# The residual of a two-layer block: identity products against a copy through memory

## The reference

```
def reference(x, seq2, lengths, expert, ...):
    y = x + attention(x, seq2, lengths) @ Wo + bo            # layer 1
    h = gelu(y @ W1 + b1)                                    # exact Gelu, 2048 wide
    shared = h @ W2 + b2                                     # 384 columns
    own    = h @ We[expert] + be[expert]                     # 128 columns, by batch
    return y + concat([shared, own], axis=-1)                # layer 2
```

## Time and profile before

| | |
|---|---|
| Median of 3 runs | 1981.19 us (1977.24 to 1981.42) |
| The profiled execution | 1981.18 us |
| Its span, first to last instruction | 1979.3 us |
| Granted clock of TensorE, mean | 0.984 of full speed |
| PE busy | 1909.4 us (96%), 8032 products |
| DVE busy | 976.5 us (49%), 1437 instructions |
| ACT busy | 825.8 us (42%), 1418 instructions |
| DMA | 122.15 MB moved |

### The profile page before, as it was taken

The page is one execution under the profiler, slowest core; times in us unless marked ns, Lnnn a source line. Parts: engine busy times, 40 slices in busy tenths (PEclk is TensorE's granted clock), DMA queues, the critical chain, the costliest instruction groups (busy, mean ns, idle before and its releaser), DMA issues.

```text
span 1979.3 us, 25912 instructions
## 1 busy us (share of the span) xinstructions
PE 1909.4 (96%) x8032; PEld 1329.4 (67%) x8032; DVE 976.5 (49%) x1437; ACT 825.8 (42%) x1418; POOL 178.6 (9%) x140
## 2 busy tenths in 40 slices
PE   6999999999999999999999799999999999999997
PEld 5655655656556556556565368888888888888886
DVE  4576585675775775866756663323232323232311
ACT  3354455454454544554544544232323232323222
POOL 3021030030120210300200100000000000000000
PEclk8999999999999999999999879999999999999999
DMA  6151243332331512432321432221212121212111
GB/s 139 33 113 43 68 84 77 60 80 53 76 79 38 117 38 65 90 76 59 75 59 43 142 100 80 35 52 31 54 29 56 27 58 25 60 23 62 21 27 22
DMA packets 337243, 122.15 MB, mean 62 GB/s; under 512 B 285642, under 2 KB 304074, under 8 KB 337170
## 3 DMA queue, kind: packets, MB, share of 16 engines
q1 hardware_dynamic: 336658, 120.83, 28.4%
q10 hardware_dynamic: 512, 0.53, 0.2%
HBM read 53.63 MB, written 16.79 MB: 36 GB/s over the span
## 4 chain that ended last, share of the span: by engine, by line
PE 88%; DVE 5%; issue 3%; SPq 2%; ACT 1%; DMA 1%; POOL 0%; DVEq 0%; ACTq 0%
PE ps_proj L1109 17%; PE ps_av L1185 11%; PE ps_max L1139 6%; PE ps_av L1061 6%; PE ps_av L1063 6%; PE ps_av L1062 6%; PE ps_score L1173 6%; PE ps_proj L1061 3%; PE ps_max L1063 3%; PE ps_score L1063 3%; PE ps_max L1062 3%; PE ps_score L1062 3%; PE ps_score L1061 3%; PE ps_max L1061 3%; PE ps_proj L1062 3%; PE ps_proj L1063 3%
## 5 line engine op out<-in xcount | busy, mean ns | idle before, releaser
L618 ACT ACTIVATE p_f<-ps_score 128x512 f32<-128x512 f32 x512 | 305.2, 598 | 457.4 <-PE ps_score L1173 439.5
L838 DVE TENSOR_REDUCE m_col<-ps_max 128x1 f32<-128x512 f32 x512 | 332.3, 685 | 258.3 <-PE ps_max L1139 257.0
L994 DVE TENSOR_TENSOR h_lo<-h_f,h_hi 128x512 fp32r<-128x512 f32 x128 | 88.3, 690 | 481.2 <-ACT h_hi L729 481.1
L1185 PE MATMUL ps_av<-p_f,v_st 128*64 128x512 f32 x1024 | 255.5, 620 | 0.0
L1173 PE MATMUL ps_score<-stacks 99*128 99x512 f32 x512 | 216.6, 425 | 10.2 <-ACT p_f L618 10.2
L1109 PE MATMUL ps_proj<-in_hi,w_hi 128*128 128x512 f32 x512 | 208.4, 407 | 10.7 <-POOL in_lo L510 7.4
L1139 PE MATMUL ps_max<-stacks 97*128 97x512 f32 x512 | 185.9, 421 | 26.5 <-DVE m_col L838 19.2
L1109 PE MATMUL ps_proj<-in_lo,w_hi 128*128 128x512 f32 x512 | 207.6, 406 | 0.0
L1109 PE MATMUL ps_proj<-in_hi,w_lo 128*128 128x512 f32 x512 | 207.2, 405 | 0.0
L1061 PE MATMUL ps_av<-y_hi,w_hi 128*128 128x512 f32 x512 | 199.4, 390 | 1.5 <-DVE y_lo L990 1.5
L1063 PE MATMUL ps_av<-y_hi,w_lo 128*128 128x512 f32 x512 | 199.2, 389 | 0.0
(11 more groups left out here) (126 smaller groups left out, 2803.0 us busy)
## 6 DMA issues: line engine op xcount, KB each, us to landing
stacks<-parts SPq DMA_DIRECT2D x384, 128.0 KB
raw<-in_x_dram SPq DMA_DIRECT2D x128, 64.0 KB, 2.2
raw<-in_fside_BxSxS_dram SPq DMA_DIRECT2D x128, 64.0 KB, 2.2
attn_scratch<-num SPq DMA_DIRECT2D x32, 256.0 KB, 2.4
x_raw<-in_x_dram SPq DMA_DIRECT2D x128, 64.0 KB, 2.1
a_raw<-attn_scratch SPq DMA_DIRECT2D x32, 256.0 KB, 3.4
we_raw<-in_L_cond_We_dram SPq DMA_DIRECT2D x32, 256.0 KB, 2.8
out_dram<-z_t SPq DMA_DIRECT2D x128, 64.0 KB, 1.9
```

Of the source, the lines that this page charges most:

```text
L618: act.activation(p_f[:, i % FLIGHT], ps_score[i % 2][:, :], ACT.Exp, scale=SCALE).then_inc(p_made, 1)
L838: dve.tensor_reduce(m_col[:, n % C, n // C:n // C + 1], ps_max[n % 2][:, :], AX.X, ALU.max).then_inc(max_made, 1)
L994: dve.tensor_tensor(h_lo[:, m % 2], h_f[:, :], f(h_hi[:, m % 2]), ALU.subtract).then_inc(h_lo_made, 1)
L1185: pe.matmul(ps_av[j // 2][at:at + 2 * DH, :], v_st[:, t, HG * g + j, :], p_f[:, i % FLIGHT], start=(t == 0), stop=(t == C - 1)).then_inc(a ...
```

## The change

The identity products go. What they added comes in another way:

- SP stores each `y_f` in memory (`keep_residual`, into a new tensor `resid_scratch`, 256 KB a tile).
- SP fetches it into `z_f`, the buffer of the result (`fetch_residual`). The tiles 0 and 1 of a batch are fetched ahead; the tiles 2 and 3 when `z_f` is free, which is when the turn two tiles earlier has been done.
- DVE evicts the output bank with bias and residual in one operation, in place in `z_f` (`result` moves from ACT to DVE).
- The output banks are started by the first output product (`m` = 0), which now waits for `z_made`.
- `x_t` goes; x is turned into `y_f`, which has two buffers now. A turn of x waits for the store of the `y` two tiles earlier.

```
+            def keep_residual(b, c):
+                sp.wait_ge(y_f_made, C * b + c + 1)
+                sp.dma_start(resid_dram[bass.ds(b, 1), c].rearrange("o p s -> (o p) s"), y_f[:, c % 2]).then_inc(y_stored[c % 2], DMA)
+            def fetch_residual(b, c):
+                wait(sp, z_t_made, C * b + c - 1)
+                sp.wait_ge(y_stored[c % 2], DMA * (2 * b + c // 2 + 1))
+                sp.dma_start(z_f[:, c % 2], resid_dram[bass.ds(b, 1), c].rearrange("o p s -> (o p) s")).then_inc(y_back[c % 2], DMA)
...
+                if first:
+                    sp.wait_ge(w2_lo_made, W2S)
+                fetch_residual(b, 0)
+                fetch_residual(b, 1)
+                if not last:
                     residual(b + 1, 0)
                     expert_weights(b + 1, 1)
                     expert_weights(b + 1, 2)
                     for c in range(1, C):
                         residual(b + 1, c)
+                        keep_residual(b + 1, c - 1)
+                    keep_residual(b + 1, C - 1)
                 for c in range(C):
+                    if c + 2 < C:
+                        fetch_residual(b, c + 2)
                     result(b, c)
...
             def turn_x(b, c):
                 n = C * b + c
                 dve.wait_ge(x_landed, (P // QUAD) * DMA * (n + 1))
-                wait(dve, y_f_made, n)
-                dve.transpose(x_t[:, :], x_raw[:, :]).then_inc(x_made, 1)
+                wait(dve, y_lo_made, n - 1)
+                wait(dve, y_stored[c % 2], DMA * (2 * b + c // 2))
+                dve.transpose(y_f[:, c % 2], x_raw[:, :]).then_inc(x_made, 1)
...
+            def result(b, c):
+                dve.wait_ge(out_mm, KH * (b + 1))
+                if c == CS:
+                    dve.wait_ge(be_landed, DMA * (b + 1))
+                dve.wait_ge(y_back[c % 2], DMA * (2 * b + c // 2 + 1))
+                dve.scalar_tensor_tensor(out=z_f[:, c % 2], in0=ps_out[c][:, :], scalar=bias_2[:, c:c + 1],
+                                         in1=z_f[:, c % 2], op0=ALU.add, op1=ALU.add).then_inc(z_made, 1)
...
                 for c in range(C):
+                    result(b, c)
                     turn_result(b, c)
...
-                    pe.matmul(ps_out[c][:, :], ident[:, :], y_hi[:, c], start=True, stop=False)
-                    pe.matmul(ps_out[c][:, :], ident[:, :], y_lo[:, c], start=False, stop=False)
...
+                    if m == 0:
+                        wait(pe, z_made, C * (b - 1) + c + 1)
+                    mm = three(ps_out[c][:, :], left, (h_hi[:, m % 2], h_lo[:, m % 2]), m == 0, m == KH - 1)
```

More of the change, by code:

```diff
@@ L42, in cond_resid_program @@
     attn_dram = nc.dram_tensor("attn_scratch", (B, C, P, S), F32, kind="Internal").ap()
+    resid_dram = nc.dram_tensor("resid_scratch", (B, C, P, S), F32, kind="Internal").ap()
     mask_dram = nc.dram_tensor("mask_scratch", (B, S), F32, kind="Internal").ap()
@@ L139, in cond_resid_program @@
         x_raw = sb2("x_raw", [P, S])
-        x_t = sb2("x_t", [P, S])
+        y_f = sb2("y_f", [P, 2, S])
         a_hi = sb2("a_hi", [P, C, S], F32R)
@@ L144, in cond_resid_program @@
         y_lo = sb2("y_lo", [P, C, S], F32R)
-        y_f = sb2("y_f", [P, S])
         h_f = sb2("h_f", [P, S])
@@ L217, in cond_resid_program @@
         y_f_made, y_hi_made, y_lo_made = sem("y_f_made"), sem("y_hi_made"), sem("y_lo_made")
+        y_stored = [sem(f"y_stored{r}") for r in range(2)]
+        y_back = [sem(f"y_back{r}") for r in range(2)]
         h_mm = sem("h_mm")
@@ L441, in _ @@
             residual(0, 2)
+            keep_residual(0, 0)
             residual(0, 3)
+            keep_residual(0, 1)
             w2_piece(2)
@@ L445, in _ @@
             w2_piece(3)
+            keep_residual(0, 2)
             expert_weights(0, 2)
+            keep_residual(0, 3)
             for n in range(4, W2S):
@@ L720, in y_high @@
                 wait(act, h_mm, KH * b)
-                act.copy(y_hi[:, c], y_f[:, :]).then_inc(y_hi_made, 1)
+                act.copy(y_hi[:, c], y_f[:, c % 2]).then_inc(y_hi_made, 1)
             def hidden(b, m):
@@ L729, in hidden @@
                 act.activation(h_hi[:, m % 2], ps_av[m % 2][:, :], ACT.Gelu, bias=bias_1[:, m:m + 1]).then_inc(h_hi_made, 1)
[L731 to L738, removed]
             act.wait_ge(small_landed, 4 * DMA)
@@ L769, in rows @@
                         y_high(b + 1, c)
-                for c in range(C):
-                    result(b, c)
             batches(act, rows)
@@ L983, in y_out @@
                 dve.wait_ge(x_made, n + 1)
-                wait(dve, y_lo_made, n)
-                dve.scalar_tensor_tensor(out=y_f[:, :], in0=ps_proj[c % 2][:, :], scalar=bias_o[:, c:c + 1],
-                                         in1=x_t[:, :], op0=ALU.add, op1=ALU.add).then_inc(y_f_made, 1)
+                dve.scalar_tensor_tensor(out=y_f[:, c % 2], in0=ps_proj[c % 2][:, :], scalar=bias_o[:, c:c + 1],
+                                         in1=y_f[:, c % 2], op0=ALU.add, op1=ALU.add).then_inc(y_f_made, 1)
             def y_low(b, c):
                 dve.wait_ge(y_hi_made, C * b + c + 1)
-                dve.tensor_tensor(y_lo[:, c], y_f[:, :], f(y_hi[:, c]), ALU.subtract).then_inc(y_lo_made, 1)
+                dve.tensor_tensor(y_lo[:, c], y_f[:, c % 2], f(y_hi[:, c]), ALU.subtract).then_inc(y_lo_made, 1)
             def hidden_low(b, m):
@@ L1272, in hidden @@
                     mm.then_inc(h_mm, 1)
-            def residuals(b):
-                for c in range(C):
-                    wait(pe, z_made, C * (b - 1) + c + 1)
-                    pe.matmul(ps_out[c][:, :], ident[:, :], y_hi[:, c], start=True, stop=False)
-                    pe.matmul(ps_out[c][:, :], ident[:, :], y_lo[:, c], start=False, stop=False)
             def outputs(b, m, first):
@@ L1289, in outputs @@
                         pe.wait_ge(we_lo_made, 4 * b + m // 4 + 1)
-                    mm = three(ps_out[c][:, :], left, (h_hi[:, m % 2], h_lo[:, m % 2]), False, m == KH - 1)
+                    if m == 0:
+                        wait(pe, z_made, C * (b - 1) + c + 1)
+                    mm = three(ps_out[c][:, :], left, (h_hi[:, m % 2], h_lo[:, m % 2]), m == 0, m == KH - 1)
                 mm.then_inc(out_mm, 1)
@@ L1304, in rows @@
                     hidden(b, m, range(C - 1, C))
-                residuals(b)
                 for m in range(KH):
```

## The result

| | before | after |
|---|---|---|
| median of 6 runs each, us | 1979.55 (1977.24 to 1981.42) | 1998.38 (1997.42 to 2000.78) |
| ratio after / before, 95% | | 1.0101 (1.0090 to 1.0111) |
| profiled execution, us | 1981.18 | 2000.78 |
| its span, us | 1979.3 | 1999.0 |

The direction was forecast, the size was not: 1986.0 with a range up to 1994.0. The profiled execution after is the slowest of its six, by 2.4 us over the median.

The account below looks back on a forecast made before the run. TensorE, busy for 100.00 of 100 us in the second half, was taken to bound the kernel. First batch +0.4, seven changes of batch +3.5 and tail +0.9 gave +4.8 us on 1981.18: 1986.0, range 1978.5 to 1994.

Parts of the forecast that it names:

- What goes: TensorE loses eight residual products in each of eight batches, 1.86 us a batch: 14.9 us if nothing else were late.
- what is late next: At a change of batch hidden tile 2 waits for ACT's second Gelu of tile 0, about 0.83 us.
- The chain over DVE and SP: At seven changes of batch, results, SP's issues and the fourth turn delay the low half: +0.5 us each, +3.5 us.
- the transfers: Two 256 KB fetches among a batch's outputs push the eighth output by 0.2 us, between 0 and 0.83.
- P - R: From the start of a batch's first result (R) to the next batch's first output product (P): forecast 10.15 us.
- the last step: From the fourth turn to the start of the next batch's first output product: forecast 1.33 us.
- rival D: TensorE's waits drop its clock to the 1.2 GHz level at seven changes of batch: +24 us, 2005; chance 0.05.
- The first batch: Turns of x 2 and x 3 wait for the stores of y, so hidden tile 2 starts later: +0.4 us.
- The tail: Behind the last product, SP starts 0.13 later, the fourth output 0.55 later, plus 0.2 for the transfer: +0.9 us.
- A: DMAs cheap, only the two issues cost, and the first batch's stores land early: +2.7 us, 1984; chance 0.27.
- B: SP's issue and the fetches hide fully because the waits for z_t and y overlap: -6.7 us, 1974.5; chance 0.10.
- C: Fourth y's fetch lands late behind outputs; fourth turn 1.0 us later in seven places and tail: +12.8, 1994; chance 0.16.

Follow-up runs that it names:

- v2: v1 with hidden tile 0 done whole before tile 1 on TensorE, and the next batch's first low half made before the last two turns on DVE: 1965.97 us.
- x6b: The changed kernel with the two late fetches of a batch cut to 64 of 512 columns, issues still on SP: 1985.09 us, ratio 1.0033 to before.
- x5b: The changed kernel with the two late fetches of a batch issued by ACT instead of SP, bytes as they are: 1983.73 us, ratio 1.0027 to before.
- v1: The changed kernel with the third and fourth y fetched early, mid-batch, into a_raw, none between the outputs: 1973.32 us, ratio 0.9975 to before.

## Why the prediction was wrong, step by step

**What goes, and what is late next.** Right. The eight products were put at 1.86 us, and v2, which doesn't wait in a change of batch, is 1.87 faster a batch. The wait of hidden tile 2 for the Gelu was forecast at 0.83 and is 0.83 (1386.14 to 1387.20, less a pace).

**The chain over DVE and SP.** This is the step that failed, by the size of one term, the transfers. The mechanism is the forecast one: the two fetches push the eighth output, the fourth turn waits for it, the low half stands behind the turn, TensorE behind that. P - R was to be 10.15 us and is 10.91. The terms: issue 6.84 for 6.69, the transfer 2.65 for 2.13, the last step 1.42 for 1.33. So the term "I take 0.2" for the transfers, between 0 and 0.83, measured 0.69, near the upper end. Its reason, that work and issue time are almost equal, used the mean share of the engines over the stretch; but a fetch that is issued in the midst of outputs makes those behind it land late, also when the mean leaves room. x6b confirms it: with seven eighths of the bytes gone and the issues left, the chain is 10.15. With the landing later, a change of batch became +1.45 instead of +0.5. Of the 0.95 between them 0.76 are the chain's; most of the rest is one place, the first change: there the first result starts 1.3 us after the last output product instead of 0.4, since it stands on DVE behind the low half of the fourth y, and ACT, which made it before, had no such queue. The prediction had put the start of the result at no change.

```profile
1278.26 0.69 DVE L1005 TENSOR_TENSOR y_lo<-y_f,y_hi 128x512 fp32r<-128x512 f32 x1 [0.69 <-ACT y_hi L747]
1278.87 0.74 DVE L1017 SCALAR_TENSOR_TENSOR z_f<-ps_score,bias,z_f 128x512 f32<-128x512 f32 x1
```

Seven times 0.95 is +6.6 us over the forecast, 1992.6 by this alone, and with the clock's 9.6 us 2002.2; the profiled execution took 2000.78, with a first half that was 1.3 us shorter.

**The clock, rival D.** It was given 0.05 and came true in six of seven places, though at half its price: 1.6 us a place, 9.6 us for the 19 that the rival had, which took twelve slow products at each of seven places where there were 7 or 8 at six. The reason against it was the wait of 1.50 us at 1182.91 after which the products went on at full pace. That gap, 1.9 us from start to start, was too short to tell: every fall stands behind one of 2.2 to 2.7 us, which the forecast chain would not have had. So the two errors are not independent: had the chain been as forecast, the gap would have been 1.5 us, as in x6b and x5b, and in their 13 changes with gaps of 1.0 to 1.6 us the clock stayed up. The Trainium skill, "TensorE: Matmul & The Clock Gate", Part 1, speaks of a fall after idleness; the falls agree with that, each stands behind a wait, and the traces add that a wait of some 2 us is enough in 12 of 17 places.

**The first batch.** Right: +0.3 for +0.4. The turns of x 2 and x 3 wait for the stores of `y` as said, at 1174.49 and 1179.78. The second half starts 1.31 us earlier in this trace, so these are 1175.80 and 1181.09 where 1175.9 and 1181.2 were forecast:

```profile
1174.49 0.71 DVE L891 STREAM_TRANSPOSE y_f<-x_raw 128x512 f32<-128x512 f32 x1 [2.04 <-DMA resid_scratch<-y_f]
1179.78 0.71 DVE L891 STREAM_TRANSPOSE y_f<-x_raw 128x512 f32<-128x512 f32 x1 [2.26 <-DMA resid_scratch<-y_f]
```

**The tail.** The sum was right and the way to it was not. From the first result of the last batch to the end are 13.6 us for 12.7, +0.9 for +0.9. But the third turn comes only 0.24 later relative to the first result (1991.33 - 1985.34 for the earlier trace rows), not 0.88, and the fourth 1.77 later (9.00 for 7.23); the outputs behind it then meet an SP queue that is empty, and give 0.9 back. The chain that ended last shows the fourth turn's cause, the landing of the eighth output, after and then before (start, length, what):

```profile
1991.65 2.60 DMA out_dram<-z_t
...
1994.34 0.71 DVE z_t L1024
```

```profile
1971.76 2.00 DMA out_dram<-z_t
...
1973.86 0.71 DVE z_t L1000
```

It is the same mis-sized term as in the changes of batch, 0.6 us here, where no loads of a next batch are in flight.

**The other rivals.** A (only the issues cost) is near what x6b is, with the bytes taken away; with them it isn't: 1.0033 in x6b, 1.0101 in the change. Its price was too low even so, +2.7 us are a ratio of 1.0014, below x6b's interval. B (faster) did not come, and v1 shows what it would have taken: the fetches away from the outputs. C (the fourth fetch late) is right in so far as DVE waits for `z_f` before results three and four, but its row is followed by one for `z_t` each time, 1.09 and 0.91 us at 1380, so the fetch was not what came last.

**The range** ended at 1994, and 1998.4 is beyond it: it took in the upper end of the transfer term alone or C, but not that term together with a part of D.

## What to carry over

A transfer that is put into a queue of outputs is priced by how much later those behind it land, and an issue that stands ahead of them by its full length; where both can be moved to a time in which the queue is empty, as in v1, the way through memory is nearly free. Where a change takes work from the busiest engine and leaves it waits, look at the granted clock behind them: here, behind a gap of 2.2 to 2.7 us, six of seven places cost 1.6 us more in slow products. And when one wait is removed without gain, look for the one that it covered: here each of two orders alone gave nothing, and both gave 7 us.

## What the runs showed of the hardware that was not expected

- Two fetches of 256 KB among outputs of 64 KB moved the outputs' median landing from 1.9 to 2.4 us over the whole program, and from 1.96 to 2.65 at the place that counts; cut to 32 KB they moved it to 2.07.
- In the second half TensorE's clock fell behind gaps of 2.2 to 2.7 us in 12 of 17 places, and behind none of 1.9 us or less. Behind the changes of batch it came back after 7 or 8 products at 0.43 us.
- Issuing two DMAs from ACT instead of SP was worth 14.6 us in the median, 0.7%, though it takes only 0.9 us off the chain at each of seven places: 9.6 us of it are the clock's in the profiled execution.
